# Decoder layer with experts: a reordered attention body with two subtractions on GpSimd, and expert weights in rows of 1 and 2 KB

## What is computed

```
x = x + self_attn(layernorm(x))
x = x + cross_attn(layernorm(x), ctx, ctx)
x = x + ffn(layernorm(x))

self_attn:  q = (x * sigmoid(sum|x|)) @ Wq;  k, v = split(x @ Wkv)
            qk = q k^T / sqrt(32) + alibi;  qk = where(allowed, -1e9, qk)
            out = softmax(qk) @ v @ Wo + bo          # 16 heads, 4 KV heads
cross_attn: softmax(q k^T / sqrt(512)) v             # 32 heads, 8 KV heads, no projections
ffn:        top 4 of 32 experts in 2 of 4 groups, capacity 128 rows an expert
            expert: (silu(b @ w1) * (b @ w3)) @ w2   # 512 -> 256 -> 512
            plus a shared expert of width 512
```

## Time and profile before

| | |
|---|---|
| median of 3 runs | 1081.57 us (1080.55 to 1083.35) |
| profiled execution, its own time | 1084.14 us |
| its span, first to last instruction | 1082.3 us |
| mean granted TensorE clock | 0.929 |
| busy share PE, DVE, ACT, POOL | 86%, 53%, 32%, 28% |
| chain that ended last, by engine | PE 56%, DVE 20%, DMA 7%, issue 6%, ACT 4%, POOL 3% |
| DMA queues, share of 16 engines | q1 26.9%, q0 8.1% |
| body 4 | 353.4 to 442.3 us |
| expert phase, scatters | 864.8 to 1082.3 us |

### The profile page before, as it was taken

The page is one execution under the profiler, slowest core; times in us unless marked ns, Lnnn a source line. Parts: engine busy times, 40 slices in busy tenths (PEclk is TensorE's granted clock), DMA queues, the critical chain, the costliest instruction groups (busy, mean ns, idle before and its releaser), DMA issues.

```text
span 1082.3 us, 16193 instructions
## 1 busy us (share of the span) xinstructions
PE 927.7 (86%) x6123; PEld 565.7 (52%) x6168; DVE 572.7 (53%) x1300; ACT 349.3 (32%) x699; POOL 303.6 (28%) x306
## 2 busy tenths in 40 slices
PE   5376899889988989898998898987999899988990
PEld 4335535645754754674574475463577455534540
DVE  2334945857757756784785785784342122212220
ACT  4020064255246326316424523524410122211120
POOL 4001000110240240142024024014215054565674
PEclk9578589899999999998999999998999999999895
DMA  4902202302300400330240230071233499989643
GB/s 135 315 2 78 59 3 67 91 3 65 93 23 23 128 10 2 95 102 2 67 111 23 61 97 3 5 266 63 87 148 89 162 322 320 328 263 308 142 62 35
DMA packets 73248, 115.14 MB, mean 106 GB/s; under 512 B 12482, under 2 KB 47584, under 8 KB 73168
## 3 DMA queue, kind: packets, MB, share of 16 engines
q1 hardware_dynamic: 55236, 94.42, 26.9%
q0 software_dynamic: 14480, 16.55, 8.1%
q10 hardware_dynamic: 3456, 3.15, 1.0%
HBM read 70.90 MB, written 16.88 MB: 81 GB/s over the span
## 4 chain that ended last, share of the span: by engine, by line
PE 56%; DVE 20%; DMA 7%; issue 6%; ACT 4%; POOL 3%; SPq 2%; another core or an unknown queue 1%; POOLq 0%; DVEq 0%; ACTq 0%
PE qa L1620 7%; DVE mxx L1027 5%; PE qa L1285 4%; DMA out<-arena,half_ids 4%; PE qx L1371 4%; PE pt L1203 4%; PE qa L1203 4%; PE qx L1607 4%; PE qa L1489 4%; ACT arena L628 3%; PE qx L1427 3%; PE vb L1438 3%; SPq L364 2%; PE qa L1456 2%; PE qa L1319 2%
## 5 line engine op out<-in xcount | busy, mean ns | idle before, releaser
L628 ACT ACTIVATE arena<-qx 128x512 f32<-128x512 f32 x256 | 148.7, 601 | 160.4 <-PE qx L1427 131.6
L1027 DVE TENSOR_REDUCE mxx<-qx 128x2 f32<-128x512 f32 x256 | 168.2, 685 | 36.5 <-PE qx L1371 34.7
L490 POOL TENSOR_TENSOR rstd<-mv,power 128x2 f32<-128x2 f32 x24 | 16.8, 701 | 449.1 <-DVE mv L855 449.1
L628 ACT ACTIVATE arena<-qa 128x512 f32<-128x512 f32 (+2 forms) x125 | 67.4, 540 | 209.7 <-PE qa L1620 100.8
L1427 PE MATMUL qx<-arena 98*128 98x512 bf16 x256 | 97.4, 404 | 34.5 <-ACT arena L628 23.0
L1620 PE MATMUL qa<-arena 128*128 128x512 f32 x256 | 117.6, 603 | 1.1 <-ACT arena L628 1.1
L1371 PE MATMUL qx<-arena 96*128 96x256 bf16 x512 | 103.3, 291 | 16.4 <-DVE mxx L1027 14.7
L1074 DVE RECIPROCAL rd<-va 128x192 f32<-128x192 f32 x32 | 43.5, 1358 | 95.4 <-PE va L1484 95.4
L1438 PE MATMUL vb<-arena 128*32 128x256 f32 x1024 | 85.6, 407 | 1.2 <-ACT arena L628 0.2
L615 POOL DMA_INDIRECT out<-arena,half_ids x44 | 68.6, 1558 | 62.9 <-DMA out<-arena,half_ids 29.0
L1371 PEld LDWEIGHTS qx<-arena 96*128 96x128 bf16 x512 | 45.9, 102 | 61.8 <-DVE mxx L1027 33.6
(11 more groups left out here) (201 smaller groups left out, 1563.7 us busy)
## 6 DMA issues: line engine op xcount, KB each, us to landing
arena<-in_L_ffn_w SPq DMA_DIRECT2D x96, 512.0 KB
qs<-arena SPq DMA_DIRECT2D x24, 384.0 KB, 5.0
arena<-arena SPq DMA_DIRECT2D x72, 128.0 KB, 2.4
res<-in_x SPq DMA_DIRECT2D x8, 512.0 KB, 8.0
xnd<-arena SPq DMA_DIRECT2D x8, 512.0 KB
ks<-arena SPq DMA_DIRECT2D x48, 64.0 KB, 2.0
arena<-arena SPq DMA_DIRECT2D x48, 64.0 KB, 2.0
arena<-arena ACTq DMA_DIRECT2D x24, 128.0 KB, 3.1
```

Source lines behind the costliest of these rows:

```text
L628: nc.scalar.activation(dst, src, func, **kw).then_inc(s[signal], 1)
L1027: v_.reduce_max(mxx[:, col:col + 3:2], xbank[v % 2].rearrange("p (h n) -> p h n", h=2), AX.X).then_inc(s["x_max"], 1)
```

## The change

The numbers that set the order in the bodies, three pieces of code that stand elsewhere, two subtractions that go from DVE to POOL, and the layout of the expert weights:

```diff
-        AT_SELF = (17, 18, 19, 21, 22, 24, 25, 27)
-        AT_HALF, AT_ROWS, AT_SLOTS = 17, 29, 23
+        AT_SELF = (15, 17, 18, 20, 21, 23, 24, 26)
+        AT_HALF, AT_ROWS, AT_SLOTS = 17, 28, 15
...
-        AT_OUT, AT_NORM, AT_FIRST = 20, 25, 28
+        AT_OUT, AT_NORM, AT_FIRST = 20, 27, 25
...
             def expert_in(e):
-                    sp.dma_start(h13[r][:, a], w[e].rearrange("(p c) f -> p c f", c=DC)).then_inc(wg_in[r], 16)
-                sp.dma_start(h2[r], w2[e].rearrange("(p c) d -> p c d", c=2)).then_inc(wg_in[r], 16)
+                    sp.dma_start(h13[r][:, a], w[e].rearrange("(c p) f -> p c f", c=DC)).then_inc(wg_in[r], 16)
+                sp.dma_start(h2[r], w2[e].rearrange("(c p) d -> p c d", c=2)).then_inc(wg_in[r], 16)
...
+                if a:
+                    pool.wait_ge(s["q_hi"], k + 1)
+                    nc.gpsimd.tensor_tensor(ql, qf, qh.bitcast(F32), ALU.subtract).then_inc(s["q_split"], 1)
                 for v in range(XU):
+                    if a and v == AT_CONTEXT + 6:
+                        pool.wait_ge(s["c_mid"], k + 1)
+                        nc.gpsimd.tensor_tensor(kp[2], kr, kp[1], ALU.subtract).then_inc(s["c_split"], 1)
...
-                        if n and v == 15:
+                        if n and v == 18:
                             norm_apply(1, k + 1, xn1)
-                        if n and v == 16:
+                        if n and v == 19:
                             token_sums(k + 1, 0)
                             token_sums(k + 1, 1)
-                        if n and v == 18:
+                        if n and v == 20:
                             token_sums(k + 1, 2)
...
                     norm_apply(2, k, xn2)
+                    if n:
+                        token_weights(k + 1)
...
                 if x:
                     cross_out(1)
-                if n:
-                    token_weights(k + 1)
...
-                        if k in FIRST_PIECE and k > 2:
-                            wait_evicted(pe, FIRST_PIECE[k] + 1)
+                    if u == 1 and k in FIRST_PIECE and k > 2:
+                        wait_evicted(pe, FIRST_PIECE[k] + 1)
...
                     for v in range(LEAD):
+                        for n_ in HELD[v] if v < len(HELD) else ():
+                            shared_slot(n_)
                         if v < 2:
                             pe.wait_ge(s["x_max"], k * XU - 1 + v)
                         cross(v)
-                        for n_ in HELD[v] if v < len(HELD) else ():
-                            shared_slot(n_)
...
                             pe.wait_ge(s["xn1"], k + 2)
+                            pe.wait_ge(s["ln2_stats"], k + 1)
                             transpose_norm(xn1, qa, "x_t")
...
-                rows = fetched[e % FETCH].rearrange("p (n c) -> p c n", c=DC)
+                rows = fetched[e % FETCH].rearrange("p (c n) -> p c n", c=DC)
...
-                    op = tr(va[:, c * P:c * P + P], he[e % 2].rearrange("p (n c) -> p c n", c=2)[:, c, :], ident[:])
+                    op = tr(va[:, c * P:c * P + P], he[e % 2].rearrange("p (c n) -> p c n", c=2)[:, c, :], ident[:])
```

More of the change, by code:

```diff
@@ L977, in queries @@
                                      ).then_inc(s["q_scaled"], 1)
-                def queries_low():
-                    dve.wait_ge(s["q_hi"], k + 1)
-                    v_.tensor_tensor(ql, qf, qh.bitcast(F32), ALU.subtract).then_inc(s["q_split"], 1)
                 def context_rem():
@@ L985, in context_rem @@
                     v_.tensor_tensor(kr, va[:, 0:S], kp[0], ALU.subtract).then_inc(s["c_rem"], 1)
-                def context_low():
-                    dve.wait_ge(s["c_mid"], k + 1)
-                    v_.tensor_tensor(kp[2], kr, kp[1], ALU.subtract).then_inc(s["c_split"], 1)
                 def self_max(u):
@@ L1031, in _ @@
                                 queries()
-                            elif v == AT_QUERY[3] + 3:
-                                queries_low()
                             elif v == AT_CONTEXT + 3:
                                 context_rem()
-                            elif v == AT_CONTEXT + 6:
-                                context_low()
                             if v in AT_SELF:
```

## The result

The changed kernel takes 1103.4 us in the median of 4 runs (1099.55 to 1114.25), the kernel before 1082.46 beside it. The ratio is 1.0209, with an interval of 1.0154 to 1.0265: slower by 21 us, where 27 us faster had been forecast. The profiled execution has a span of 1101.1 us.

What follows compares the result with a forecast made beforehand. PE, nearly always busy, bounds the bodies; POOL's late scatter-adds end the expert phase. Bodies -9 and weights -18 sum to -27 against 1084.1: 1057, or 1055 us for the median; own range 1044 to 1071, overall range 1044 to 1083.

Steps and rivals of the forecast that it cites:

- The bodies: All body changes with the edges: -9 us, between -16 and +2; bodies 3 to 6 -1.95 each, body 7 -0.1.
- AT_NORM 25 to 27: End of a body, token weights right behind the second norm: gain 0.4 us a body, from 0.7 lost to 1.6 gained.
- The sign of being wrong that the prediction names: Body 4 taking more than 88.9 us would show the forecast for the bodies wrong.
- HELD steps: Two shared steps moved before cross(0), filling PE's 1.14 us wait for DVE: gain 0.65 us, ends 0 and 1.14.
- ACT's norm later: norm_apply(1) and token sums three steps later, removing PE's 0.90 us stall before a projection: gain 0.90, ends 0 and 0.90.
- Together 0: AT_SELF two steps earlier, subtractions on POOL: DVE's relief balanced by a new q wait; ends -0.8 and +0.8 us a body.
- forecast wait for the q rows: First self step at v=15: q rows land about 375.3, late ones 376.3, PE arrives 374.9; stall 0.4 to 1.4 us.
- So nothing: Slots' eight indirect issues moved from v=23 to v=15: no effect, since the shared output behind them waits at v=23 anyway.
- The edges: Body 0 +0.9 us, going into body 1 -2.5, bodies 1 and 2 together -1.2, body 8 +1.5.
- The gain would be in who goes next: Expert phase, rows of 1 and 2 KB: scatters wait less behind weights, so POOL keeps up better; -18 us, -10 to -27.8.
- rival B: Engines give q0 the same part whatever the rows' size; only the 10% counts: 1080 us, 1074 to 1092, chance 0.23.
- B's price: Small rows raise q1's 100 us of full engines to 105 to 110; POOL reaches the same expert 5 to 10 us later.

Runs made afterwards that it cites:

- e9: Kernel before with AT_NORM = 27 and AT_FIRST = 25 alone (plus a wait for the second norm's sums): 1115.59 us, ratio 1.0330.
- e8: Changed kernel keeping AT_NORM = 27 and AT_FIRST = 25, but DVE's cross_out(0) ahead of the second norm's application: 1055.99 us, ratio 0.9915.
- e4: Changed kernel with AT_NORM = 25 and AT_FIRST = 28 again: 1051.16 us, ratio 0.9883 to the kernel before.
- e5: Changed kernel, unedited, measured again on another chip: 1074.07 us, ratio 1.0124 to the kernel before.
- e7: Changed kernel with AT_NORM = 25, AT_FIRST = 28 and AT_SLOTS = 23 again: 1056.92 us, ratio 0.9939 to the kernel before.
- e6: Kernel before, unedited, profiled on another chip: 1065.55 us, one run.
- e16: Changed kernel with norms, slots, self scores and rows as before, and both subtractions back on DVE: 1057.59 us, ratio 0.9792 to the kernel before.
- e15: Changed kernel with norms, slots, self scores and rows (AT_SELF, AT_ROWS) as before, subtractions still on POOL: 1058.34 us, ratio 0.9804 to the kernel before.
- e14: Changed kernel with AT_NORM = 25, AT_FIRST = 28, AT_SLOTS = 23, on a chip with the idle time: 1066.55 us, ratio 0.9875 to the kernel before.
- e10: Changed kernel with norms, AT_SELF and AT_ROWS as before, slots still at 15, subtractions on POOL: 1070.32 us, ratio 0.9896 to the kernel before.
- e13: Changed kernel, unedited, once more on a chip with the idle time: 1098.81 us, ratio 1.0193 to the kernel before.
- e2: Changed kernel with the weights in rows of 4 KB again: 1079.69 us, ratio 1.0160 to the kernel before.
- e1: Kernel before with the new weights' layout and matching transposes alone: 1059.64 us, ratio 0.9953.
- e18: Changed kernel with norms, slots, self scores as before, w1 and w3 in rows of 512 B: 1045.00 us, ratio 0.9832 to the kernel before.
- e17: Changed kernel with norms, slots, self scores as before, weights in rows of 4 KB with strided transposes: 1051.67 us, ratio 0.9877 to the kernel before.

## Why the prediction was wrong

**The bodies.** -9 was forecast, +30 came. The step that failed is "AT_NORM 25 to 27": "the 1.12 us wait for the second norm goes" is right, and "DVE runs without a gap from there" is where it broke. I had followed DVE's chain as it ran before and held it fixed, and looked for what waits for xn2, but did not ask what `cross_back(1)` at v=26 waits for. That wait (for x2, the count of `cross_out`) cost nothing before, because PE stood at v=25 for a result that comes 1.0 us earlier in the same DVE queue, and then transposed; so it was in no row. The exchange took its cover away: 34 us in e9, 18 to 22 back in e8, and by the ratios some 26 in e4 against e5. None of the rivals had it. The sign of being wrong that the prediction names came true: body 4 took 92.8 us, over 88.9.

**The clock.** The sum counted waits at their own length. In the first measurement bodies 3 to 6 lost 8.5 us in idle time and 16 us in slower matmuls; between e5 and e8 it was 11.3 and 6.3. So in these two comparisons more idle time costs 2.9 and 1.6 times its length.

**HELD steps, ACT's norm later.** Right: both waits are gone, 23.0 us of waits for ACT became 2.8. Not all of that is theirs: with norms and slots back these waits are 8.7 us in e7, where e6 has 16.0. That they are worth something shows in e16 only together with the rest, 0.9792.

**Self scores earlier, subtractions on POOL.** "Together 0". The forecast wait for the q rows came (0.95 us in body 4, 9.3 over seven bodies, of 0.4 to 1.4 each forecast) and POOL's subtraction takes 1.81 us, 1.9 forecast. That the wait fits is luck in part: the sum's own terms (369.0 to 369.3, and 5.0 to 6.0 behind) give 374.0 to 375.3 and not 375.3 to 376.3. The missing time is there in the run: 1.25 us pass in body 4 between the end of POOL's subtraction at 377.21 and the start of the transfer that ends the wait at 378.46, in which SP issues; the landing then took 6.04. The relief of DVE that was to balance it didn't: e16 against e15 gives nothing for it, and e15 against e14 gives 8 us for putting the self scores back. Mis-sized by these 8 us.

**Slots.** "So nothing" looked at POOL's own queue alone. This is the second step that failed. On chips with the idle time it costs DVE in the first pass, 12 us by e10 and e15; on the others v=15 is 6 us better (e4, e7). The first measurement was on a chip with it. What norms and slots take together is 3.2% there (e13, e14) and 1.9% without it (e5, e7).

**The edges.** Body 0 took 1.8 us less, 1.6 forecast. Bodies 1 and 2, forecast at -1.2, took 3.2 us more. In body 8 PE waits 3.4 us for a transfer, 1.5 forecast; slower weights are not why, since e2 with rows of 4 KB has 3.3.

**The weights.** "The gain would be in who goes next" failed: -18 was forecast, e1 gives -4. q0's part of the engines' time did not follow the rows' size: 28.6, 27.5 and 28.1%. That is what rival B said. The Trainium skill ("DMA: Bandwidth & Descriptors", "Queues, rings and completion order") has an engine drain a packet of descriptors before it changes queue. The prediction took B's outcome from this; it doesn't follow, since a packet of as many but smaller rows would leave q0 a larger part, and no run here shows how many rows one holds. B's price, 5 to 10 us for 10% of packet time, failed as well. The tail of the changed kernel was 11 us shorter in the first profile. Small rows make 3 of it: 227.3 us in e1 against 230.5 in e6, 223.2 in e5 against 226.0 in e2. The other part comes with the changed bodies and at either size of rows, 4.5 and 4.1 us by the same four. The later start alone is not why: e4 starts 5 us before e1 and takes 223.5. The cause stays open.

The changed kernel isn't the best of its parts. e15 (norms, slots and self scores as before; weights, held steps, ACT's norm and token weights as changed) takes 0.9804 of the kernel before, 22 us less; with rows of 512 B on another chip 0.9832, where rows of 4 KB take 0.9877.

## What to carry to other kernels

When a step moves past another on an engine that runs its program in order, look at every wait of the steps it passes, those that cost nothing before above all, and ask what had covered them. Price a new wait with the clock that follows it. And price a change of transfer sizes by the bytes that the mixed queues move in a stretch, not by the sum of packet times.

## What was not expected of the hardware

During and just behind the last of eight indirect transfers DVE stood idle for 0.7 to 3.6 us at a time, and ACT longer, on some chips and not on others, and the kernel before takes 1081 us on the first kind and 1062 to 1064 on the second. What holds them is not shown, nor that it makes all of this difference. Rows of 512 B for two thirds of the weights were no slower than rows of 4 KB: 322 GB/s in the mixed stretch (e18), 323 and 324 with 4 KB (e6, e17).
